# Joined weight half-banks spread over the first routing and the gap ahead of the second layer

## The chip, the cores and the metric

The kernel runs on one NeuronCore of a Trainium2 chip. The metric is the time of one launch in device microseconds; the median of three runs is the time of a kernel. A core has TensorE (PE in the profile), VectorE (DVE), ScalarE (ACT), GpSimd (POOL) and SyncE (SP, here the issuer of most DMAs), which run each its own instruction stream and meet at semaphores.

## The reference

Two layers over 1250 nodes of width 1024, all in float32. Each layer adds to x a graph layer and an attention layer of its normed input, and then a mixture of experts:

```python
edge_index = jnp.stack([src, dst])
xn = _layernorm(x, axis=-1)
x = x + _L0_gnn_ref(xn, edge_index, L0_gnn_W, L0_gnn_b) + _L0_mix_ref(xn[None], ...)[0]
x = x + _L0_ffn_ref(_layernorm(x, axis=-1)[None], L0_ffn_router_gate, ...)[0]
xn = _layernorm(x, axis=-1)
x = x + _L1_gnn_ref(xn, src, dst, ...) + _L1_mix_ref(xn[None], L1_mix_Wq, ..., L1_mix_P)[0]
x = x + _L1_ffn_ref(_layernorm(x, axis=-1)[None], ...)[0]
```

What matters here are two parts. The first expert layer routes: softmax of 8 scores for each token, the best two experts, and in each expert the 391 tokens of largest gate; the kernel must rank the tokens before it can gather any. The attention of the second layer maps queries and keys through a block of 64 features a head before anything else:

```python
q = split_heads(x @ Wq.T + bq)
k = split_heads(x @ Wk.T + bk)
q_prime = _feature_map(q, P)      # relu(q @ P^T) / 8
k_prime = _feature_map(k, P)
```

So Wq and Wk can each be multiplied by P once, ahead of time. These products are the joined weights.

## The kernel before

The work is one long sequence of stages, and the order in each engine's stream is the order in the program text. Matrix products are done as three products of high and low parts (`three`, L515 to L517). Weights come in units of 128 x 2048 (1 MB): SP loads a unit into one of two buffers `WS`, ACT casts the high part into one of two buffers `WH` (`next_unit`, L1494), DVE subtracts to get the low part (L1913), and PE uses the unit. SP's load of a unit waits until the unit two before it has been split.

The joined weights are computed on PE by `joined(n)`, n = 0 to 31 (`JOINED`): block j = n // 2 is one block of 128 rows of Wk (j < 8) or Wq (j >= 8), loaded by SP into `natural(j)`, eight places that the blocks share and that lie in the same memory as the gathered tokens of the experts. A half n is four matmuls against the features `pbd` (L622) into one half of the PSUM tile `PA`. ACT copies each half to `joined_stage(j)`, a ring of `JRING` = 4 places (L1796), SP stores the finished block to the DRAM tensors `pw_d` (`store_joined`, L1196) and then loads the Wq block into the place that is free. Later `linear(pw_d[0])` and `linear(pw_d[1])` load them as weight units.

The first routing, between the graph layer and the experts of layer 0, runs so. DVE computes the gates from the scores (up to L2451) and signals `gates_ready`; PE transposes them (L1041), DVE copies them out (L2458 to L2462); a sum gives the count of each expert. Then for each of 20 groups of tokens PE makes a matrix of all gates (L1056) and DVE compares and counts (L2481 to L2486): the rank loop. From the ranks DVE builds one-hot rows (L2075), PE multiplies them into token numbers (L698), DVE writes `tidx` (L2080), POOL gathers the tokens of expert 0 and, once all joined halves are done, of expert 1 (`gather`, L1423). DVE prepares the gate weights (L2084, L2086) and PE multiplies them (L706). PE then waits for the last copy of a joined half and enters `experts(0)`, which begins with eight register reads and a branch on them, and with the transposes of the gathered tokens (L724).

PE does the joined halves in between: 0 to 5 ahead of the wait for `gates_ready`, 6 to 8 between the transposes, 9 to 21 in the rank loop, 22 to 27 after it, 28 between the two token products, 29 to 31 after them. ACT enters `experts(0)` when all stores have landed.

After the experts PE multiplies the biases by the features (L633, L638), ACT copies them out (L1802, L1804), waits for the last scatter of the experts' results (POOL, L1440) and reads the result back for the second layer; `joined_biases` is the last that the experts' stage leaves on PE before `linear_rows("v1")`.

## Time and profile before

| what | value |
|---|---|
| median of 3 runs | 3187.97 us (3185.45 to 3194.71) |
| the profiled execution | 3187.38 us, of it the span 3185.4 us |
| PE busy | 3002.7 us, 94% of the span |
| DVE, ACT, POOL busy | 62%, 40%, 15% |
| chain that ended last | PE 86%, DVE 7%, issue 2%, DMA 2% |
| granted clock of PE, mean | 0.969 |

The chain is followed back from the last instruction: at each step to what released it. "Issue" is time in which an engine waited for nothing that the profile shows. A busy share is a mean over stages; what a stage is bound by is read in its own window. The routing is short, from about 1024 to 1125 us of the span.

### The profile page before, as it was taken

Reading aid. Unit: us, or ns where it says so; the run is one execution under the profiler, and the core shown is the slowest. Engines: PE = TensorE matmul, PEld = TensorE weight load, DVE = VectorE, ACT = ScalarE, POOL = GpSimd, SP = SyncE. Lnnn points to the kernel's source line nnn. Section 1 sums busy time; section 2 is a strip of 40 time slices with the busy share of each in tenths; the row PEclk is TensorE's granted clock in tenths of the full one; section 3 lists DMA queues with packets and bytes.
Section 4 is the critical chain, followed back from the end, with each engine's and each line's share of the span. In section 5 each row is a group of like instructions: output and inputs, shape, how many; then the busy total and the mean of one; then the engine's idle time right before and its main releaser. Section 6 shows DMA issues by size and latency. Waiting matters only on the chain.

```text
span 3185.4 us, 53094 instructions
## 1 busy us (share of the span) xinstructions
PE 3002.7 (94%) x22248; PEld 2765.1 (87%) x22248; DVE 1983.2 (62%) x3497; ACT 1270.0 (40%) x2176; POOL 462.9 (15%) x328
## 2 busy tenths in 40 slices
PE   8899999999999889999979999999999999979997
PEld 7898898379987778889879999899999999968997
DVE  6986477977876733544456666676355653655665
ACT  3354045444431233433335444544134531424554
POOL 1034443444000111110100000000000000002222
PEclk9999999999999989999989999999999999988999
DMA  7322112123034755755551101363322333248997
GB/s 250 131 59 44 1 16 59 1 51 74 15 86 151 244 142 157 202 154 141 146 148 61 44 27 44 113 153 89 95 78 71 91 90 98 72 137 239 272 281 212
DMA packets 280544, 361.71 MB, mean 114 GB/s; under 512 B 41283, under 2 KB 239465, under 8 KB 278614
## 3 DMA queue, kind: packets, MB, share of 16 engines
q1 hardware_dynamic: 188137, 228.87, 23.6%
q0 software_dynamic: 43312, 77.14, 12.0%
q10 hardware_dynamic: 48829, 51.86, 5.7%
q8 instruction: 203, 3.33, 0.4%
q14 instruction: 63, 0.52, 0.1%
HBM read 273.01 MB, written 84.79 MB: 112 GB/s over the span
## 4 chain that ended last, share of the span: by engine, by line
PE 86%; DVE 7%; issue 2%; DMA 2%; ACT 1%; ACTq 1%; SPq 0%; POOL 0%; DVEq 0%; POOLq 0%
PE PV L515 18%; PE PV L516 18%; PE PV L517 18%; PE PV L685 5%; PE PS L515 3%; PE PS L517 3%; PE PS L516 3%; PE PV L1009 3%; DVE b L2237 2%; PE PA L724 1%; PE PV L915 1%; PE PV L955 1%; PE PA L930 1%; PE PS L930 1%; PE PS L524 1%
## 5 line engine op out<-in xcount | busy, mean ns | idle before, releaser
L515 PE MATMUL PV<-WH,b_split 128*125 128x256 f32 (+2 forms) x4028 | 1174.5, 292 | 41.6 <-DVE b_split L1924 37.1
L516 PE MATMUL PV<-WH,b_split 128*125 128x256 f32 (+2 forms) x4028 | 1159.4, 288 | 2.4 <-issue 2.4
L517 PE MATMUL PV<-WH,b_split 128*125 128x256 f32 (+2 forms) x4028 | 1158.3, 288 | 2.6 <-issue 2.6
L1924 DVE TENSOR_TENSOR b_split<-b,b_split 128x500 fp32r<-128x500 f32 x1008 | 668.7, 677 | 444.5 <-ACT b_split L1504 435.9
L1504 ACT CAST b_split<-b 128x500 fp32r<-128x500 f32 x1008 | 608.4, 613 | 740.9 <-PE PV L517 697.0
L515 PEld LDWEIGHTS PV<-WH,b_split 128*125 128x125 f32 (+2 forms) x4028 | 754.0, 187 | 63.7 <-issue 32.8
L516 PEld LDWEIGHTS PV<-WH,b_split 128*125 128x125 f32 (+2 forms) x4028 | 757.0, 188 | 12.5 <-issue 2.6
L517 PEld LDWEIGHTS PV<-WH,b_split 128*125 128x125 f32 (+2 forms) x4028 | 754.1, 187 | 14.2 <-issue 3.0
L1913 DVE TENSOR_TENSOR WH<-WS,WH 128x1024 fp32r<-128x1024 f32 x292 | 344.4, 1221 | 125.5 <-ACT WH L1494 124.3
L1494 ACT CAST WH<-WS 128x1024 fp32r<-128x1024 f32 x292 | 291.5, 1049 | 182.6 <-PE PV L685 141.1
L1399 POOL DMA_INDIRECT at_d<-ecnt,eidx x168 | 273.9, 1630 | 391.9 <-DMA at_d<-ecnt,eidx 366.7
L1423 POOL DMA_INDIRECT b<-xn_d,tidx x66 | 65.6, 994 | 1611.5 <-issue 1300.1
L515 PE MATMUL PV<-b_split,WH 128*128 128x250 f32 (+3 forms) x816 | 247.5, 303 | 8.2 <-issue 5.9
L516 PE MATMUL PV<-b_split,WH 128*128 128x250 f32 (+3 forms) x816 | 242.5, 297 | 0.0
L517 PE MATMUL PV<-b_split,WH 128*128 128x250 f32 (+3 forms) x816 | 242.0, 297 | 0.0
L685 PE MATMUL PV<-WH,b_split 125*128 125x250 f32 x1600 | 196.4, 286 | 9.6 <-DVE b_split L2040 7.6
L685 PEld LDWEIGHTS PV<-WH,b_split 125*128 125x128 f32 x1600 | 193.5, 194 | 12.5 <-issue 8.0
L515 PE MATMUL PS<-b_split,WH 128*128 128x256 f32 (+2 forms) x496 | 158.6, 320 | 11.2 <-issue 8.4
L515 PEld LDWEIGHTS PV<-b_split,WH 128*128 128x128 f32 x816 | 156.7, 192 | 9.8 <-issue 9.4
L2105 DVE TENSOR_TENSOR b_split<-PA,b_split 128x256 fp32r<-128x256 f32 (+1 forms) x192 | 83.8, 466 | 127.4 <-ACT b_split L1626 127.3
L516 PEld LDWEIGHTS PV<-b_split,WH 128*128 128x128 f32 x816 | 156.9, 192 | 0.2
L517 PEld LDWEIGHTS PV<-b_split,WH 128*128 128x128 f32 x816 | 156.7, 192 | 0.0
(295 smaller groups left out, 3570.3 us busy)
## 6 DMA issues: line engine op xcount, KB each, us to landing
WS<-in_L_ffn_w SPq DMA_DIRECT2D x46, 1024.0 KB, 7.7
WH<-at_d SPq DMA_DIRECT2D x15, 1093.8 KB
WS<-in_L_ffn_gate_w SPq DMA_DIRECT2D x16, 1024.0 KB, 6.6
WS<-in_L_ffn_up_w SPq DMA_DIRECT2D x16, 1024.0 KB, 6.5
WS<-in_L_ffn_down_w SPq DMA_DIRECT2D x16, 1024.0 KB, 5.1
b<-key_d POOLq DMA_DIRECT2D x4, 2560.0 KB, 8.9
WS<-in_L_mix_Wv SPq DMA_DIRECT2D x8, 1024.0 KB, 7.8
WS<-in_L_mix_Wo SPq DMA_DIRECT2D x8, 1024.0 KB, 7.1
```

The lines of the kernel that those rows point to most:

```text
L515: pe.matmul(o, a[0], b[0], start=start, stop=False, **kw)
L516: pe.matmul(o, a[0], b[1], start=False, stop=False, **kw)
L517: return pe.matmul(o, a[1], b[0], start=False, stop=stop, **kw)
L685: mm = pe.matmul(bank[:, 0:AC], part[:, j, f * P:(f + 1) * P].bitcast(dt), at[:, j, :], start=(j + a == 0), stop=(j + a == NT))
L1009: mm = pe.matmul(bank[0:R, :], at[:, j, t * R:(t + 1) * R], part[:, j, half * HALF:(half + 1) * HALF].bitcast(dt), start=(j + a == 0), sto ...
L1399: pool.indirect_dma_start(out=at_d, out_offset=bass.IndirectOffsetOnAxis(ap=eidx[:, g:g + 1], axis=0), in_=ecnt[:, g:g + 1], in_offset=Non ...
L1423: pool.indirect_dma_start(out=ffn_xe(layer, b)[0:r, t, :], out_offset=None, in_=xn_d, in_offset=bass.IndirectOffsetOnAxis(ap=tidx[0:r, c:c ...
L1494: act.copy(WH[:, u.place % 2, a:a + UNIT // 2], WS[:, u.stage % 2, a:a + UNIT // 2])\
L1504: act.copy(hi, src).then_inc(xh_done, 1)
L1913: ve.tensor_tensor(WH[:, u.place % 2, UNIT + a:UNIT + a + UNIT // 2], WS[:, u.stage % 2, a:a + UNIT // 2], WH[:, u.place % 2, a:a + UNIT / ...
L1924: ve.tensor_tensor(lo, src, hi.bitcast(F32), ALU.subtract).then_inc(xl_done, 1)
L2105: ve.tensor_tensor(xeT[:, 1, k, :], bank, xeT[:, 0, k, :].bitcast(F32), ALU.subtract).then_inc(t_free, 1)
```

## The change

The halves are laid out anew. None runs ahead of `gates_ready`; 0 to 2 stand between the transposes, 3 to 16 in the rank loop, 17 to 23 after it, 24 and 25 between the token products. PE then enters the experts after 26 halves (`ROUTED`). The other six, blocks 13 to 15, run after the experts, ahead of the biases. Their Wq blocks, which lay where the tokens of the odd experts are gathered, are loaded by SP after the last transposes of expert 7, and their stores come with the loads of the second layer. The gather for expert 1 waits for 26 halves. The stage ring has three places, so that the late blocks don't touch memory in use. ACT casts the next weight unit ahead of its copies, no longer after six of them, and waits for the late stores ahead of the pieces of the second layer. A block is stored as it lies, 4 KB a partition, and a unit is loaded by two DMAs of one block each, with a semaphore more.

```diff
-JRING = 4
+JRING = 3
 JOINED = 2 * 2 * KD
+ROUTED = 2 * 13
...
-            pe.wait_ge(sm_in, 1)
-            for n in range(6):
-                joined(n)
             pe.wait_ge(gates_ready, 1)
...
-                joined(6 + a)
+                joined(a)
...
-                for m in range(9 + 13 * n // 20, 9 + 13 * (n + 1) // 20):
+                for m in range(3 + 14 * n // 20, 3 + 14 * (n + 1) // 20):
                     joined(m)
             pe.wait_ge(rank_used, rank_ops[2 * NT - 1])
-            for n in range(22, 28):
+            for n in range(17, 24):
                 joined(n)
-            row_tokens(0, lambda: joined(28))
-            for n in range(29, JOINED):
+            row_tokens(0, lambda: [joined(n) for n in range(24, ROUTED)])
+            pe.wait_ge(jw_copied, ROUTED)
+            experts(0)
+            for n in range(ROUTED, JOINED):
                 joined(n)
-            pe.wait_ge(jw_copied, JOINED)
-            experts(0)
             joined_biases()
...
-            def store_joined():
-
-                for j in range(2 * KD):
+            def natural_query(j):
+                sp.dma_start(natural(j), A["L1_mix_Wq"][j * P:(j + 1) * P, :]).then_inc(nat_in[j], 16)
+
+            def store_joined(blocks):
+
+                for j in blocks:
                     sp.wait_ge(jw_copied, 2 * (j + 1))
-                    pr = j % KD
-                    sp.dma_start(pw_d[j // KD][:, pr * P:(pr + 1) * P].rearrange("(k p) c -> p k c", p=P),
-                                 joined_stage(j).rearrange("p (k c) -> p k c", c=P)).then_inc(jw_st[j % JRING], 16)
-                    if j < KD:
-                        sp.dma_start(natural(j), A["L1_mix_Wq"][j * P:(j + 1) * P, :]).then_inc(nat_in[j], 16)
+                    sp.dma_start(pw_d[j // KD][j % KD], joined_stage(j)).then_inc(jw_st[j % JRING], 16)
+                    if j + KD < ROUTED // 2:
+                        natural_query(j)
+
+            def linear_joined(w, vec=None):
+
+                for q in range(NQ):
+                    u = units[n_unit[0]]
+                    n_unit[0] += 1
+                    sp.wait_ge(wl_done, 2 * (u.stage - 1))
+                    for a in range(2):
+                        sp.dma_start(WS[:, u.stage % 2, :].rearrange("p (k n) -> p k n", k=KD)[:, :, a * P:(a + 1) * P],
+                                     w[2 * q + a].rearrange("p (k c) -> p k c", c=P))\
+                          .then_inc(ws_half[u.stage % 2] if a == 0 else ws_full[u.stage % 2], 16)
+                    if vec is not None:
+                        bias(vec, q)
...
-            store_joined()
+            store_joined(range(ROUTED // 2))
...
+            sp.wait_ge(*gather_end[0, E - 1])
+            for j in range(ROUTED // 2 - KD, KD):
+                natural_query(j)
             for q in range(NQ):
                 if q == 2:
+                    store_joined(range(ROUTED // 2, 2 * KD))
                     sp.wait_ge(jw_copied, JOINED + 2)
...
-            linear(pw_d[0], pb_d[0, :])
-            linear(pw_d[1])
+            linear_joined(pw_d[0], pb_d[0, :])
+            linear_joined(pw_d[1])
...
                 if layer == 0:
-                    pool.wait_ge(jw_full, JOINED)
+                    pool.wait_ge(jw_full, ROUTED)
...
-            for slot in range(JRING):
-                act.wait_ge(jw_st[slot], 16 * (2 * KD // JRING))
+            def joined_stored(blocks):
+                for slot in range(JRING):
+                    act.wait_ge(jw_st[slot], 16 * len(range(slot, blocks, JRING)))
+
+            next_unit()
+            for n in range(ROUTED):
+                joined_copied(n)
+            joined_stored(ROUTED // 2)
             experts(0)
+            for n in range(ROUTED, JOINED):
+                joined_copied(n)
...
             next_unit()
+            joined_stored(2 * KD)
             hi_pieces(wide_pieces(B2), lead=lead_x2, order=by_pair)
```

## Rows read from the trace of the kernel before

**Rows 1.** Chain of waits, 1018 to 1150 us: start, duration, what.

```profile
1058.67 1.42 PE PV L1056 x6
...
1097.44 5.84 PE PA L622 x48
1103.29 1.79 PE PV L698 x20
...
1107.13 4.97 PE PV L706 x40
1112.10 4.69 PE PA L622 x24
...
1117.41 7.37 issue
```

**Rows 2.** Timeline of PE: start, duration, instruction, in brackets the idle before.

```profile
1042.01 8.37 PE L622 MATMUL PA<-b 128*128 128x128 f32 x48 [3.65 <-DMA b<-in_L_mix_Wk]
...
1055.85 1.23 PE L1041 MATMUL PV<-ident,RB 125*8 125x125 f32 x10
```

**Rows 3.** Timeline of DVE: start, duration, instruction, in brackets the idle before.

```profile
1044.60 0.24 DVE L2451 TENSOR_TENSOR RB<-RB 125x80 f32<-125x80 f32 x1
1051.27 0.67 DVE L2460 CAST b_split<-PV 8x500 fp32r<-8x500 f32 x1 [6.42 <-PE PV L1041]
...
1102.00 2.41 DVE L2075 TENSOR_TENSOR b_split<-RB,rowno 125x490 fp32r<-125x490 f32 x4
1105.11 0.19 DVE L2080 TENSOR_SCALAR tidx<-PV 98x32 int32<-98x32 f32 x1 [0.70 <-PE PV L698]
```

**Rows 4.** Timeline of POOL: the memset and the last gather of expert 0.

```profile
1038.43 4.26 POOL L1405 MEMSET b_split<- 128x5000 f32 x1 [227.60 <-PE PA L552]
...
1109.86 0.95 POOL L1423 DMA_INDIRECT b<-xn_d,tidx  x1 [0.30 <-issue]
```

**Rows 5.** Windows: busy of PE, PEld, DVE, ACT, POOL, then clock, DMA share, GB/s.

```profile
1040.50:1041.00 0.50, 0.00 (x0) 0.00 (x0) 0.50 (x9) 0.00 (x0) 0.50 (x1) 0.90 1.01 393
1047.50:1048.00 0.50, 0.50 (x5) 0.50 (x5) 0.00 (x0) 0.49 (x1) 0.00 (x0) 0.78 1.08 442
1119.00:1119.50 0.50, 0.00 (x0) 0.00 (x0) 0.00 (x0) 0.00 (x0) 0.27 (x1) 0.90 0.98 261
1133.00:1133.50 0.50, 0.50 (x5) 0.50 (x4) 0.32 (x1) 0.15 (x1) 0.00 (x0) 0.94 0.00 0
```

**Rows 6.** DMA: landings of gathers at 1109.86 and 1120.83; listing 1020 to 1130 us.

```profile
DMA to landing us min/median/max: 5.9/5.9/5.9
DMA to landing us min/median/max: 12.4/12.4/12.4
...
pw_d<-b SPq DMA_DIRECT2D x16, 512.0 KB, 3.4
b<-in_L_mix_Wq SPq DMA_DIRECT2D x8, 512.0 KB, 7.0
WS<-in_L_ffn_up_w SPq DMA_DIRECT2D x1, 1024.0 KB, 15.1
```

**Rows 7.** SP, ACT, chain and one window between the experts and the second layer.

```profile
1553.28 7.23 SPq L1178 DMA_DIRECT2D WS<-in_L_ffn_down_w  x2
...
1589.40 0.17 ACT L1804 COPY bcol<-PA 128x8 f32<-128x8 f32 x1 [1.30 <-PE PA L638]
...
1588.92 8.16 DMA x_d<-b,sidx
...
1588.00:1590.00 2.00, 1.36 (x13) 1.28 (x12) 0.00 (x0) 0.27 (x2) 1.70 (x2) 1.00 0.99 172
```

**Rows 8.** Second layer: a load of joined weights, its cast, landings of such loads.

```profile
1712.81 0.43 SPq L1178 DMA_DIRECT2D WS<-pw_d  x1
...
1744.94 1.99 ACT L1494 CAST WH<-WS 128x1024 fp32r<-128x1024 f32 x2
...
DMA to landing us min/median/max: 4.8/5.7/7.7
```

13 lines of the change are left out of this document (8 added, 5 removed).

## Prediction

> **What bounds the kernel now.** I read the page first: TensorE (PE) is busy 94% of the span and holds 86% of the chain of waits, so time is won only where that chain leaves the long runs of matmuls. Then I read the chain of waits from 1018 to 1150 us, the first routing, where all 32 half-banks of joined weights (L622, one `joined(n)` each) are computed. PE's own timeline [rows 2] shows six of them at 1042.01 for 8.37 us, after 3.65 us of waiting for the Wk blocks. The chain [rows 1] holds six more at 1097.44 for 5.84 us (0.97 each); three at 1112.10 for 4.69 us. Then the timelines of DVE and POOL in the same stretch [rows 3, 4], to see who waits behind PE; the granted clock in half-microsecond windows [rows 5]; the DMA listing and the landings [rows 6]; the chain, ACT and the DMA between the experts and the second layer, where six halves go [rows 7]; and the loads of the joined weights in the second layer [rows 8].
>
> **The profiled execution.** It took 3187.38 us for a span of 3185.4; the median of three runs is 3187.97. I work in differences against the profiled one and take them off the median.
>
> **Front of the routing.** DVE finishes the gates at 1044.60 + 0.24 = 1044.84 and then idles 6.42 us until 1051.27 [rows 3], because PE stands in the six halves until 1042.01 + 8.37 = 1050.38 [rows 2] before it transposes the gates. The change takes these six out. The other input of that step, POOL's memset, ends at 1038.43 + 4.26 = 1042.69 [rows 4], so the gates are last: PE can start at 1044.84 in place of 1050.38, 5.5 us earlier. All the halves that stay between the gates and the first rank matmul (three) are the same number as before.
>
> Against it stands the clock. It fell to half during the 3.65 us in which PE waited for Wk and came back at about 1047.7, after PE had been kept full by the six halves [rows 5]. Now PE idles some 6.5 us and meets the transposes at half clock, 1.2 GHz in place of 2.4. From 1050.38 to 1058.67 [rows 1] PE has some 6.5 us of work at full clock (30 transposes, of which ten take 1.23 us [rows 2], and three halves of 0.97); the rest of the 8.3 us is DVE's. If the clock returns about 5 us after the start, the PE work is some 2.5 us behind, of which DVE's share hides about 1: a cost of 1.5. If it returns within 3 us the cost is under 1; if only at the rank matmuls, 2 x 6.5 - 8.3 = 4.7, or a little more. I take 1.5: PE is kept nearly as full as it was by the six halves, if with smaller matmuls. Front: 5.5 - 1.5 = 4.0, between 0.5 and 5.
>
> The Trainium skill ("TensorE: Matmul & The Clock Gate", section "HAM oscillation — how this bites in real kernels") says that gaps in PE's work return it to half rate and that each burst after one begins cold. The trace agrees: the pauses of 3.65 and 7.37 us both ended at half clock [rows 5].
>
> **Rank loop.** From 1058.67 to 1097.44 DVE is busy without a break worth naming; PE does 14 halves beside it in place of 13. Where three steps in a row now carry one, PE's step is about as long as DVE's (38.8/20 = 1.94): cost 0.3, bounds 0 and 0.9 (a whole half).
>
> **Between ranks and tokens.** Seven halves in place of six: 7 x 0.97 = 6.8 us. The first token matmul follows the halves at once, at 1103.29 [rows 1], when DVE's last one-hot is still being written (1102.00 + 2.41 = 1104.41 [rows 3]); the 20 matmuls of 1.79 us end at 1105.08 and tidx is written at 1105.11. In the new order the halves end so late that nothing of this hides: cost 1.0, bounds 0 and 1.0.
>
> **Tail.** Under DVE's weights (1105.11 to 1107) two halves run in place of one. They take 1.9 us and DVE 2.0: nothing, or 0.9 if the cover is gone. After the weight matmuls (L706, 4.97) the three halves and the last copy, 1112.10 to 1117.41, fall away: 5.3. The 7.37 us "issue" behind them stays whole. In the code it is eight register reads and a branch, all behind the wait for the copies, and the first gather had landed by then: 1109.86 + 5.9 = 1115.8 [rows 4, 6]. What is late next is this gather: with tidx 2.7 earlier its last tile lands near 1113, PE wants it at 1116.8.
>
> **Ring of three and SP.** ACT now waits for the store three blocks back. A block takes 1.9 us of halves, so three take 5.8, and a store lands in 3.4 [rows 6]: covered; without cover each block would cost the difference, up to 1.5. ACT's weight cast goes ahead of its copies (2 us, in PE's pause). SP leaves the stores for the expert weights 5 us earlier or more.
>
> First routing: 4.0 - 0.3 - 1.0 + 5.3 = 8.0 us.
>
> **The six moved halves.** PE ends the experts near 1585.6, ACT its bias copies at 1589.40 + 0.17 = 1589.57 [rows 7]. With six halves of about 0.95 between them ACT ends near 1595.1. ACT's next step waits for the last scatter, 1588.92 + 8.16 = 1597.08 [rows 7]: covered by 2 us. If the halves ran at half clock this cover is gone and 3 us would come on top. Blocks 5 to 7 of Wq are read again by SP after its last expert weights, issued by 1553.28 + 7.23 = 1560.5; such a block takes 7.0 us to land [rows 6], PE wants them at 1585.6: covered by 18 us. The Wv loads queued behind them on SP wait for a buffer anyway.
>
> What is not free is the stores of blocks 13 to 15: SP issues them at about 1588, 1590 and 1592, 1.5 MB through the engines that the scatter fills to 0.99 at 172 GB/s [rows 7]. The nearest rows: the last tile of the gather that ran beside the 1 MB up_w load landed in 12.4 us, that of the one before it in 5.9, and up_w took 15.1 [rows 6]. So sharing can cost up to 6.5; down to 0 if the scatter has only latency to wait for. I take 3: only part of the stores lies ahead of the scatter's last packets. The chain runs through this landing, so it counts in full.
>
> The Trainium skill ("DMA: Bandwidth & Descriptors", section "Queues, rings and completion order") has each DMA engine take turns between its queues packet by packet. By it the scatter gives up half of the engines as long as stores are queued; a rule without it would let the scatter, issued earlier, go first and the cost be near 0.
>
> **Blocks of 4 KB a partition.** Stores get longer pieces; loads of the joined weights become two DMAs with 512 B pieces on chip. A load is issued at 1712.81, lands in 7.7 at most and is cast at 1744.94 [rows 8]: even at twice the time it is 16 us early. Nothing; the same for ACT's new waits ahead of the second layer, since the stores land before the scatter's successor loads do.
>
> **Sum.** 8.0 - 3.0 = 5.0 us: 3182.4 for the profiled execution, 3183.0 for the median.
>
> **Rivals.**
> 1. The scatter is not held. For: its landings may be latency. Against: up_w and the gather both grew. Gain 8.0: 3180.0.
> 2. The clock stays low through the front. For: a longer pause, and the half-clock spell from 1119 to 1133 outlasted the first 8 us of work [rows 5]. Against: at 1047.7 it returned after 5.7 us. Front 0.5 in place of 4.0: gain 1.5, 3186.5.
> 3. The gather becomes the late one: gather(1) now follows at once, no longer held by the last half, beside the stores. With 12.4 in place of 5.9 its predecessor's last tile lands at 1107.2 + 12.4 = 1119.6, 2.8 after PE wants it: gain 2.2, 3185.8. Against: it lies ahead of gather(1) in its queue.
> 4. Slower: the stores hold the scatter by their whole size. 1.57 MB at the 172 GB/s of that stretch are 9.1 us; 8.0 - 9.1 = 1.1 lost, 3189.1. It decides from 8.0 us of delay on. Against: these bytes need no read of the target, and the nearest row shows 6.5.
>
> **Chances.** Forecast 0.50, rivals 0.20, 0.12, 0.10 and 0.08. The clock at either routing end may add or take 2.5 us (the half-clock spell at the start of the experts can fall otherwise). With it the ends are a gain of 11.5 (rival 1 with a good clock) and a loss of 2: 3176.5 to 3190. A change of 0.3% is 9.6 us, about what a measurement tells from none. Faster by more: half of rival 1, a tenth of the forecast and a little of the rest, 0.17; slower by more: part of rival 4, 0.05; within: 0.78.
>
> **What would show it.** Right: the gate transposes begin within 0.5 us of gates_ready; DVE's 6.4 us gap is gone; the first expert transpose (L724) comes 7 to 9 us earlier; the last scatter before the second layer lands in 10 to 13 us, not 8.2. Wrong: a gap of DVE in the rank loop, PE released into the experts by a gather, ACT's bias copies after the scatter, or any wait of ACT for a joined load. The prediction fails most easily at the scatter and at the clock.

## The result and the profile after

The changed kernel takes 3169.2 us (median of 8 runs, 3165.7 to 3171.2) against 3186.2 us (median of 8, 3180.1 to 3194.7): a ratio of 0.9943, interval 0.9931 to 0.9954. It is 17 us faster where 5 were forecast, and 7 us under the low end of the range. Its profiled execution took 3169.48 us, of it the span 3167.7, against 3187.38 and 3185.4 before.

The difference of the two spans, 17.7 us, stage by stage (each border is the start of the named instruction of PE in either trace):

| stage | before | after | difference | forecast |
|---|---|---|---|---|
| start to the last scores | 1038.1 | 1035.9 | -2.2 | 0 |
| last scores to first gate transpose | 12.1 | 6.8 | -5.3 | -5.5 |
| to the first rank matmul | 8.5 | 9.0 | +0.5 | +1.5 |
| to the first token product (L698, now L701) | 44.3 | 45.4 | +1.1 | +1.3 |
| to the first expert transpose (L724, now L727) | 21.8 | 15.0 | -6.8 | -5.3 |
| experts, to the end of PE's expert matmuls | 460.8 | 448.8 | **-12.0** | **0** |
| to the key products of the second layer | 186.9 | 191.6 | +4.7 | +3 |
| to the end | 1412.9 | 1415.2 | +2.3 | 0 |

The first and the last row are no work of the change. Over the profiles of all kernels below whose code is the same up to there, the last scores began between 1035.3 and 1042.0 us; and the last row came to 1410.7 us in a second profile of the changed kernel and to 1411.9 in one of the kernel before. So single rows of this table are good to a microsecond or two where they are short, and to a few where they are long. The routing and the stage behind the experts came out near the forecast. Most of what the forecast lacked is one line, the experts, none of whose instructions the change touches.

The chain of waits of the changed kernel, answering [rows 1] (start, duration, what):

```profile
1090.61 6.74 PE PA L625 x56
1097.34 1.68 PE PV L701 x20
...
1103.79 8.20 DMA b<-xn_d,tidx
```

The halves behind the rank loop are seven, 6.74 us. The three halves and the 7.37 us of "issue" that ended the routing are gone from the chain; it ends with the landing of a gather. PE's timeline says the same, and answers [rows 2] (in brackets the idle time before, and its releaser):

```profile
1042.69 2.25 PE L1041 MATMUL PV<-ident,RB 125*8 125x125 f32 x10 [6.53 <-DVE RB L2479]
...
1101.07 3.62 PE L709 MATMUL PV<-RB,b_split 125*98 125x32 f32 x40 [0.18 <-DVE RB L2114]
1112.13 1.54 PE L727 MATMUL PA<-ident,b 98*128 98x98 f32 x8 [7.44 <-DMA b<-xn_d,tidx]
```

DVE's timeline, answering [rows 3]: the gates are ready at 1042.63, the gap behind them is 1.51 us where it was 6.42, and `tidx` waits 1.47 us for the token product, where it waited 0.70:

```profile
1042.39 0.24 DVE L2479 TENSOR_TENSOR RB<-RB 125x80 f32<-125x80 f32 x1
1044.14 0.67 DVE L2488 CAST b_split<-PV 8x500 fp32r<-8x500 f32 x1 [1.51 <-PE PV L1041]
...
1099.05 0.19 DVE L2108 TENSOR_SCALAR tidx<-PV 98x32 int32<-98x32 f32 x1 [1.47 <-PE PV L701]
```

Windows of the changed kernel (length, busy of PE, PEld, DVE, ACT, POOL, granted clock, DMA share, GB/s), answering [rows 5]:

```profile
1047.00:1047.50 0.50, 0.50 (x5) 0.29 (x3) 0.47 (x2) 0.28 (x1) 0.00 (x0) 0.56 1.06 410
1047.50:1048.00 0.50, 0.50 (x6) 0.42 (x5) 0.50 (x2) 0.00 (x0) 0.00 (x0) 1.00 0.99 350
...
1118.00:1119.00 1.00, 1.00 (x5) 1.00 (x4) 0.44 (x1) 0.00 (x0) 0.00 (x0) 0.50 1.04 246
1119.00:1120.00 1.00, 1.00 (x8) 0.90 (x8) 0.00 (x0) 0.34 (x1) 0.00 (x0) 0.94 0.62 140
```

PE began the gate transposes at 1042.69 at half clock (1.2 GHz) and had the full one (2.4 GHz) from 1047.5, 4.8 us later; it began the experts at 1112.13 at half clock and had the full one 6.9 us later.

Between the experts and the second layer, answering [rows 7]: chain of waits, then ACT's timeline (its last line stands in the chain as well), then SP's.

```profile
1564.30 12.20 DMA x_d<-b,sidx
```

```profile
1570.36 0.17 ACT L1831 COPY bcol<-PA 128x8 f32<-128x8 f32 x1 [1.30 <-PE PA L641]
...
1587.60 1.28 ACT L1543 ACT_TABLE_LOAD   x1 [4.51 <-DVE b L2007]
```

```profile
1563.46 5.34 SPq L1199 DMA_DIRECT2D pw_d<-b  x3
```

ACT's bias copies end 9.7 us behind PE's experts (9.5 forecast) and are covered by the scatter. The scatter, with three stores of joined blocks issued from 0.8 us ahead of it on, lands in 12.20 us where it landed in 8.16. And a step stands in the chain that was not in it before: ACT's table load for the square root. The loads of the joined weights, answering [rows 8], now of half the size, land in 6.1 us at the median, where those of 1 MB took 5.7, and nothing waits for them:

```profile
WS<-pw_d SPq DMA_DIRECT2D x10, 512.0 KB, 6.1
```

**Where the 12 us of the experts went.** One window over the stage, of the kernel before and of the changed one:

```profile
1124.80:1585.60 460.80, 444.31 (x2495) 391.94 (x2496) 202.18 (x254) 169.47 (x254) 70.81 (x54) 0.98 0.57 155
```

```profile
1112.10:1560.87 448.77, 441.16 (x2495) 389.83 (x2496) 201.94 (x253) 169.44 (x254) 70.63 (x54) 0.99 0.60 164
```

The same 2495 matmuls. PE's idle time falls from 460.80 - 444.31 = 16.5 to 7.6 us, that is by 8.9, and its busy time by 3.1, at a mean clock of 0.99 in place of 0.98. What PE waited for in this stage, before and after (us in total, times, longest):

```profile
PE PV L515 <- issue: 5.9, 3, 5.3
PE PS L515 <- issue: 5.5, 2, 3.0
PE PV L517 <- issue: 2.6, 1, 2.6
```

```profile
PE PS L518 <- issue: 2.6, 1, 2.6
PE PS L520 <- issue: 1.3, 1, 1.3
PE PV L520 <- issue: 0.5, 1, 0.5
PE PV L518 <- issue: 0.5, 1, 0.5
```

PE stands still with nothing to wait for, 14.0 us before and 4.9 after. The largest stops of the kernel before, in PE's timeline and in the chain:

```profile
1149.47 0.67 PE L515 MATMUL PV<-b_split,WH 128*128 128x392 f32 x1 [5.30 <-issue]
```

```profile
1248.42 2.56 issue
...
1292.87 2.43 issue
...
1341.47 3.04 issue
```

They fall between matmuls whose data were there. For the longest that needs a second look, since DVE splits a weight unit until 1148.03, shortly before PE goes on at 1149.47, and in one of the kernels below (a_pad24) the profile names this split as the releaser of the same stop. But in the changed kernel PE begins the same matmul at 1130.88, and DVE begins that split only at 1132.42: it is of a later unit. What moves at that moment is the instruction queue. It shows 39 transfers in the stage, and each of the four stops has one. In the three shorter stops it starts within 0.3 us of the stop, takes about 1 us, and PE goes on 1.5 to 2.1 us after its end; in the longest it starts at 1146.6, 2.4 us into the stop.
```profile
q8 instruction: 1, 0.02, 11.8%
```

The longest stop also costs clock. Windows of the kernel before, columns as above:

```profile
1146.00:1148.00 2.00, 0.00 (x0) 0.00 (x0) 2.00 (x2) 0.59 (x1) 0.00 (x0) 0.68 0.79 213
...
1150.00:1152.00 2.00, 2.00 (x8) 2.00 (x7) 0.00 (x0) 0.00 (x0) 0.00 (x0) 0.50 1.08 378
...
1154.00:1156.00 2.00, 2.00 (x16) 1.96 (x14) 0.12 (x1) 0.00 (x0) 0.00 (x0) 1.00 0.00 0
```

At half clock PE did 8 matmuls in two microseconds, at the full one 16. The DMA engines were busy in most of these stops, but not in all: in the one from 1248.4 to 1251.0 their share is 0.23 in this trace.

The Trainium skill ("Runtime: NRT & Kernel Launch", section "Instruction fetch mechanics") says that each engine's instructions are fetched in blocks of 16 KiB, 256 instructions, while it executes the current ones, that the cost of crossing into a new block is mostly hidden, and that a taken branch breaks the fetching ahead. The size agrees with the 16.4 KB of a transfer here. "Mostly hidden" doesn't hold for this stage as a whole, with 13.3 us in four stops. What branches have to do with it is the last experiment's question.

So the theory behind the experiments: **the change moved 24 matmuls (six halves of four) from ahead of the experts to behind them, and thereby the place of every instruction of the experts within its block. Where the block's borders fall decides how long PE waits for the next block.** The rival: the moved work itself, or the times of the gathers, makes the experts faster.

### The profile page after: what moved, and what is told of

It is laid out like the page before. It is cut to its first block, busy times and chain, and to the rows that moved or that the text cites. A ratio compares the mean times of both kernels' runs of the same rounds, so it can differ in the third digit from the quotient of the medians.

```text
span 3167.7 us, 53105 instructions
## 1 busy us (share of the span) xinstructions
PE 2990.9 (94%) x22248; PEld 2754.0 (87%) x22248; DVE 1982.6 (63%) x3497; ACT 1270.0 (40%) x2176; POOL 468.0 (15%) x328
## 3 DMA queue, kind: packets, MB, share of 16 engines
q0 software_dynamic: 43312, 77.14, 12.1%
## 4 chain that ended last, share of the span: by engine, by line
PE 88%; DVE 6%; issue 2%; ACT 1%; DMA 1%; ACTq 1%; SPq 0%; POOL 0%; DVEq 0%; POOLq 0%
PE PV L518 18%; PE PV L520 18%; PE PV L519 18%; PE PV L688 6%; PE PS L518 4%; PE PS L520 3%; PE PS L519 3%; PE PV L1012 3%; PE PA L727 2%; DVE b L2265 2%; PE PV L918 1%; PE PV L958 1%; PE PA L933 1%; PE PS L933 1%; PE PS L527 1%
```

## The experiments

**Repeats** (b_again, a_again). Both kernels again, for what is chance.

> The kernel before, unchanged, profiled once more. Between the first expert transpose and the biases PE stood idle four times for 5.3, 2.6, 2.4 and 3.0 us with nothing to wait for, each with an instruction transfer in flight. If the stops belong to where the instructions lie, they come back at the same instructions and with about the same size; if they are chance, they come elsewhere or are smaller.

> The changed kernel, unchanged, once more: 3169 us, ratio 0.994. In its first trace only two such stops stood in the experts, 1.3 and 2.6 us. By the layout theory the same two return; by chance the sum could be anything up to the 13 us of before.

The kernel before took 3187.6 us, its stage of experts 463.2. The changed kernel took 3166.4 us, ratio 0.9937 (0.9913 to 0.9962), its stage 449.9. Large stops of similar size stood at the same places of either stage (5.5, 3.0, 2.6 and 2.1 us; 1.2 and 2.4). They belong to the program and not to the run.

**The place alone, in both directions.** Matmuls of two columns, of whose result nothing is used. In f32 each is four instructions of PE, as those of a joined half are. First at the start of PE's stream: 24 in the changed kernel (a_pad24), which puts the experts where those of the kernel before lie, and 40 in the kernel before (b_pad40), 24 + 40 = 64 matmuls or 256 instructions from the changed kernel.

```diff
             pe.wait_ge(consts, 8)
+            for _ in range(24):
+                pe.matmul(PA[0:P, 0, 0:2], ident[:, :], ones[:, 0:2], start=True, stop=True)
```

> The changed kernel with 24 small matmuls at the very start of PE, where PE is idle for the first 30 us. They cost nothing there, but put the expert instructions back to the place that they had before the change (the six moved halves are 24 matmuls). Layout theory: the stops of before return (5.3 us at the first hidden columns, 13 us in all in place of 4) and the time is 3178 us. Rival (the stop of 5.3 us came from the transfers beside it, or from chance): no change, 3169 us.

> The kernel before with 40 such matmuls at the start: the expert instructions lie as in the changed kernel, if what counts is their place within blocks of 16 KB. Layout theory: 9 us less, 3177 us. Rival: as before, 3186 us.

The changed kernel with 24: 3182.8 us, ratio 0.9989 (0.9978 to 1.0000), experts 463.1. The kernel before with 40: 3178.8 us, 0.9976 (0.9964 to 0.9987), experts 447.7. The expectation that these matmuls are free was wrong. The 24 took 10.4 us, so that PE's first transposes began at 14.5 us in place of 12.4, and the 40 took 17.2 us and put them off from 12.0 to 21.4. The last scores came 3.6 and 8.2 us later; the first of these lies within what they move by themselves (1035.3 to 1042.0), the second doesn't. But the stage of experts changed sides in both kernels.

Then the same in the routing, 40 ahead of the first joined half of the kernel before (b_gap40) or 24 ahead of the wait for the gates in the changed kernel with its table load mended (t_gap24; the mending is a_table's, below):

```diff
+            pe.wait_ge(sm_in, 1)
+            for _ in range(24):
+                pe.matmul(PA[0:P, 0, 0:2], ident[:, :], ones[:, 0:2], start=True, stop=True)
             pe.wait_ge(gates_ready, 1)
```

> The kernel before with forty matmuls of two columns (their result is used by nobody) behind PE's wait for sm_in, ahead of the first joined half, where PE waits 3.6 us for the weights of Wk in the kernel before. They shift the place of every later instruction of PE as forty such matmuls at the start of PE did (which shortened the experts from 461 to 448 us but cost 10 us at the start), and do nothing else to the routing. Theory (the place of PE's instructions sets 13 of the 17 us): the stage from the first expert transpose to the end of PE's expert matmuls is 448 us instead of 461 to 463, the routing is 0 to 3 us longer by the forty matmuls, and the whole is 3186.5 - 13.5 + 1.5 = 3174.5 us, 3172.5 to 3176.5. Rival (the forty at the start did it by something else than their place, such as by when x0's loads or the scores ran): experts 461 to 463 us, whole 3186 to 3190 us.

> The changed kernel with the table load mended as in the run on that, and twenty-four matmuls of two columns ahead of PE's wait for the gates, where PE stands idle. Their number is that of the matmuls of the six halves that the change moved behind the experts, so the experts' instructions of PE lie where those of the kernel before lie. Theory of the place: the experts' stage is 463 us instead of 449, the front is no longer than in the changed kernel (at most 1 us either way, for the clock falls later), and the whole is 3168 + 13.5 = 3181.5 us, 3179.5 to 3183.5: the gain of the moved work alone, about 5 us of 3186.5, which is what was forecast for it. Rival (the moved halves themselves make the experts faster): experts 449 us and 3168 us.

The kernel before with 40: 3184.8 us, 0.9996 (0.9984 to 1.0009), experts 446.3. The total is 10 us above the expected one, since the 40 cost 11.7 us here and not 1.5. Each took 0.39 us, nearly all at half clock. The changed kernel with 24: 3187.6 us, 1.0002 (0.9990 to 1.0015), experts 462.5. That is 6 us above the expectation; 3.2 of it is the cost of the 24 ahead of the gates, and the rest is open: the profiled execution, from which the stages are read, took 3177.6 us, 10 less than the median. The window over its experts and three of the stops in its chain (the longest, 5.3 us, is back as well, at the same matmul as in the kernel before):

```profile
1115.20:1577.74 462.54, 445.74 (x2495) 393.26 (x2495) 202.09 (x253) 169.34 (x254) 70.58 (x54) 0.97 0.60 160
```

```profile
1237.63 2.50 issue
...
1283.35 2.75 issue
...
1333.57 2.60 issue
```

They stand 122.4, 168.2 and 218.4 us behind the first expert transpose (1115.2). In the kernel before it is 123.6, 168.1 and 216.7 (from 1124.8).

**Is it the place within a block?** In the same place a whole block, 64 matmuls, and two other values, each profiled once.

 Theory of the block: every later instruction lies at the same place within its block as in the changed kernel, and the experts' stage (first expert transpose to the end of PE's expert matmuls, 448.8 us in the changed kernel, 462.5 with twenty-four) is 448 to 452 us, with the stops for issue at the instructions of the changed kernel (the largest near 204 us into the stage). Rival (any matmuls ahead of the experts lengthen the stage, or more of them more so): 462 us or above. The sixty-four cost some 22 to 25 us ahead of the gates (0.39 us each, as forty took 15.8 us in b_gap40), so that the whole is 3190 us by the theory and 3204 by the rival; the stage alone is what tells.

> As t_gap24 with twelve matmuls of two columns: 48 instructions, half of the way from the places of the changed kernel to those of the kernel before. Theory of the block, in which each block's end meets another matmul and other transfers of the weights: the stage is anything between 448 and 463 us, and its stops stand at other matmuls than in either kernel. Rival (a switch between two states by some threshold): 448 or 463 us to within 2 us, with the stops of one of the two kernels. The whole is 3168 us plus what the stage has above 449 (the twelve lie in PE's idle time).

> As t_gap24 with forty-four matmuls of two columns: 176 instructions, between the places of the kernel before (24) and the whole block (64). Theory of the block: the stage is between 446 and 465 us, with stops at other matmuls. Rival (more matmuls ahead, longer stage): above 463 us. The forty-four cost some 11 us ahead of the gates.

With 64, window and stops:

```profile
1133.60:1579.95 446.35, 439.55 (x2494) 388.23 (x2495) 201.90 (x253) 169.58 (x254) 71.35 (x55) 0.99 0.62 166
```

```profile
1292.06 1.26 issue
...
1337.93 1.31 issue
```

The short stage is back, with stops 158.5 and 204.3 us behind the first transpose (1133.6). The changed kernel has them at 158.6 and 204.5 (from 1112.1):

```profile
1270.67 1.34 issue
...
1316.62 2.63 issue
```

So what counts is neither that matmuls are added nor how many, and the remainder in blocks of 256 instructions fits. Half, a quarter or an eighth of a block as the period doesn't: 12 and 44, which lie half a block apart, differ by 10.7 us in the table. By the matmuls that stand ahead of the experts beyond those of the changed kernel:

| matmuls more | kernel | stage of experts | of it PE idle | PE busy |
|---|---|---|---|---|
| 0 | changed | 448.8 | 7.6 | 441.2 |
| 0 | a_table | 451.7 | 9.8 | 441.9 |
| 8 | a_28 | 458.7 | 13.2 | 445.5 |
| 12 | t_gap12 | 462.2 | 16.9 | 445.3 |
| 24 | before | 460.8 | 16.5 | 444.3 |
| 24 | a_pad24 | 463.1 | 17.9 | 445.2 |
| 24 | t_gap24 | 462.5 | 16.8 | 445.7 |
| 44 | t_gap44 | 451.5 | 8.5 | 442.9 |
| 64 | b_pad40 | 447.7 | 7.1 | 440.6 |
| 64 | b_gap40 | 446.3 | 6.1 | 440.2 |
| 64 | t_gap64 | 446.4 | 6.8 | 439.6 |

The kernels that are not in the table keep to their side: 462 to 463 us in b_again, b_front and b_4k (24 more), 448 to 450 in a_again, a_held, a_hoist and a_late (none more). The expectation for twelve was half wrong: three of its four large stops do not stand at other matmuls. They stand at 18.9, 163.5 and 213.9 us into the stage, where the kernel before has three of its own. The fourth, 3.05 us at 440.6, has no counterpart there. With 8 the stage lies between the two values; with 44 it is that of a_table, with one large stop (3.8 us) in place of a_table's two of 1.3 and 2.9. The whole times of the three single runs (3185.8, 3180.4 and 3177.1 us) carry the added matmuls too and say less.

**The front alone** (b_front). The kernel before with the halves of the routing spread as in the change, but the last six left behind the weight products, ahead of the experts. The places of the experts' instructions stay.

```diff
-            pe.wait_ge(sm_in, 1)
-            for n in range(6):
-                joined(n)
...
-                joined(6 + a)
+                joined(a)
...
-                for m in range(9 + 13 * n // 20, 9 + 13 * (n + 1) // 20):
+                for m in range(3 + 14 * n // 20, 3 + 14 * (n + 1) // 20):
...
-            row_tokens(0, lambda: joined(28))
-            for n in range(29, JOINED):
+            row_tokens(0, lambda: [joined(n) for n in range(24, 26)])
+            for n in range(26, JOINED):
```

> The kernel before with one part of the change alone: no half-bank ahead of the gates, 3, 14, 7 and 2 at the later places as in the change, and the last six still ahead of the experts, after the weight matmuls. The expert instructions lie as before, so the layout theory gives the stops of before and an experts stage of 461 to 463 us, not 448. The front gains 5, six halves after the weight matmuls cost 6 in place of three for 5: in all 3 to 4 us gained, 3183. If instead the front itself brought the missing gain, 3175 or less.

ACT casts the next weight unit ahead of its copies here, too. 3185.9 us, 1.0001 (0.9987 to 1.0015), where 3183 were expected: no gain is seen, though the interval leaves room for one of 4 us. Between the scores and the gate transposes it wins 5.3 us, as the changed kernel does, but six halves now stand between the weight products and the experts where there were three, and the first expert transpose comes only 0.6 us earlier against the scores. Experts 463.0. By this trace the front is worth something only with the six halves taken away.

**What releases the experts.** First the second gather held back until the experts have begun (a_held), then also PE's eight register reads moved into the rank loop (a_hoist).

```diff
                 if layer == 0:
                     pool.wait_ge(jw_full, ROUTED)
+                    pool.wait_ge(t_full, 1)
                 gather(1)
```

```diff
+                if n in (3, 5, 7, 9, 11, 13, 15, 17):
+                    pe.wait_ge(nsel_ready, 1)
+                    e = len(chosen)
+                    chosen.append(pe.value_load(nsel[0:1, e:e + 1], min_val=0, max_val=T))
                 if n >= 2:
                     pe.wait_ge(rank_used, rank_ops[n - 2])
```

> The changed kernel, but the gather for expert 1 waits until PE has turned the first bank of expert 0, so that it no longer runs beside the gather of expert 0. In the changed kernel the last tile of that gather landed in 8.2 us (5.9 before) and the first expert transpose came 7.4 us after the weight matmuls, at the very moment of landing. If the gather sets the start (rival 3 of the prediction), the transpose comes 2 us earlier and the kernel gains 2 us. If the eight register reads and the branch set it (7.4 us before as after), nothing moves: 3167 us.

> As a_held, and the eight register reads are made one by one between the steps of the rank loop. If the 7.4 us are these reads, the first transpose now waits for the gather alone, some 5 us after the weight matmuls: 2 us gained, less what the reads delay the rank loop (0 to 5 us, if each takes 0.6 us of PE). If they are the branch, nothing is gained.

3166.4 us, 0.9939 (0.9923 to 0.9956), and 3169.4 us, 0.9951 (0.9934 to 0.9967): neither differs from the changed kernel. PE's timeline of the first and of the second:

```profile
1116.72 1.54 PE L727 MATMUL PA<-ident,b 98*128 98x98 f32 x8 [5.74 <-DMA b<-xn_d,tidx]
```

```profile
1111.82 1.54 PE L727 MATMUL PA<-ident,b 98*128 98x98 f32 x8 [5.49 <-DMA b<-xn_d,tidx]
```

With the reads out of the way PE still waits 5.5 us, for the gather's landing; with them in their place it waited 5.7 us in a_held and 7.4 in the changed kernel. So what comes last there is the gather, and taking the reads away alone is worth nothing. How far behind the gather the reads would hold PE is not measured. The gather's landing moved between 4.9 and 8.2 us, also with the second gather held: that gather is not what it waits for.

**The scatter.** In a_late the three late stores are put behind the read-back of x2, so that the scatter runs without them, and ACT waits for them behind the first pair of the second layer.

```diff
                 if q == 2:
-                    store_joined(range(ROUTED // 2, 2 * KD))
...
                     sp.dma_start(gate_sb[:, :, :], A["L1_ffn_gate_w"].rearrange("(k p) e -> p k e", p=P))\
                       .then_inc(rg1_in, 16)
+                    store_joined(range(ROUTED // 2, 2 * KD))
```

> The changed kernel, but the stores of blocks 13 to 15 wait until the first rows of the result are back, and ACT waits for them after the first pair of the second layer in place of ahead of it. Theory: the last scatter lands in 8.2 us again in place of 12.2 (4 us), and ACT's table load falls back into its pause (1.3 us): 5 us less than the changed kernel, 3163. Rival: the landing of the scatter grew for another reason, and the stores now delay the rows that come back: no gain or a loss.

3177.3 us, 0.9972 (0.9959 to 0.9985): 8 us worse than the changed kernel. The scatter in the chain, and the stores in the DMA listing (the last number there is the median from issue to landing):

```profile
1565.05 8.03 DMA x_d<-b,sidx
```

```profile
pw_d<-b SPq DMA_DIRECT2D x3, 512.0 KB, 20.1
```

The scatter is back at 8.0 us: its 4 us are the stores' doing. But beside the read-back and a load of Wv the stores themselves take 20 us and become the late thing: the chain waits 19.5 us for them. The other way to less of it, a_28, is two late stores in place of three, with the two halves more behind the weight products, under the gather (the table load is mended, as in a_table below):

```diff
-ROUTED = 2 * 13
+ROUTED = 2 * 14
...
-            row_tokens(0, lambda: [joined(n) for n in range(24, ROUTED)])
+            row_tokens(0, lambda: [joined(n) for n in range(24, 26)])
+            for n in range(26, ROUTED):
+                joined(n)
```

> The changed kernel with the table load mended and four of the 32 halves instead of six behind the experts: the two others stand behind the matmuls of the combine weights, where PE waits 5 to 7 us for the gather; two joined blocks instead of three are stored beside the last scatter. Theory: the scatter lands in some 11 us instead of 11.2 to 12.2 (8.2 without late stores, plus two thirds of 4), the two halves (1.8 us) lie in the wait for the gather, so that the first expert transpose is no later than with six; 0 to 2 us of gain with the experts at the same length. But the eight matmuls move the experts' instructions by 32 places, so that their stage may be anything between 447 and 463 us: whole 3167 to 3182 us. The stage tells which. Rival: the gather waits for the two halves (pool waits for all the halves ahead of the second gather) and the first expert transpose comes 2 us later: nothing gained.

3179.5 us, 0.9971 (0.9957 to 0.9984), 10 us worse, 7 to 10 of them in the experts, which take 458.7 us by the place of their instructions. PE also stood 3.1 us for issue behind the gather's landing, ahead of the first transpose, so that this came 2 us later than without the two halves. The scatter landed in 11.18 us, no sooner than in other runs with three late stores (10.7 to 12.2). Two stores hold it as well as three, or this difference is too small to see.

**The table load** (a_table). ACT's waits for the last stores one line higher:

```diff
-            next_unit()
-            joined_stored(2 * KD)
+            joined_stored(2 * KD)
+            next_unit()
```

> The changed kernel with one wait moved: ACT's waits for the three last stores of joined weights (joined_stored(2 * KD)) stand ahead of next_unit() instead of behind it. In the changed kernel ACT's table load of 1.28 us (L1543) starts at 1587.60, when DVE's L2007 is done, because these waits and the one for the variance stand ahead of it. Theory: with the waits ahead of the weight casts the table load lies in ACT's idle time ahead of the variance again, as before the change, and the stage from the end of the experts to the key products is 1.3 us shorter than the 191.8 us of the changed kernel; 3167.9 us. The stores land before the scatter does, so that moving their wait forward holds nothing. Rival: the waits now hold the weight casts (L1515, 1.05 us, that follow the scatter), and nothing is won: 3169.2 us. No instruction of PE moves, so the experts stay at 448 to 450 us by either.

ACT's line for the square root in this kernel (durations least, median, most in ns; first and last start):

```profile
L1543 ACT ACT_TABLE_LOAD  x1: 1283/1283/1283, 1585.1 to 1585.1; - x1
```

The load now starts 4.4 us ahead of the square root that needs it (1589.5) and is gone from the chain. The stage from the end of PE's expert matmuls to the key products is 190.5 us (191.6), as expected. The time is 3168.9 us, 0.9944 (0.9924 to 0.9964): one microsecond doesn't show in medians that differ by 3.

**The 4 KB layout alone** (b_4k), with the store into whole tiles and the waits for both halves of a load.

```diff
-        pw_d = [dram("pw_d0", [D, D]), dram("pw_d1", [D, D])]
+        pw_d = [dram("pw_d0", [KD, P, D]), dram("pw_d1", [KD, P, D])]
...
-            linear(pw_d[0], pb_d[0, :])
-            linear(pw_d[1])
+            linear_joined(pw_d[0], pb_d[0, :])
+            linear_joined(pw_d[1])
```

> The kernel before with the third part of the change alone: the joined weights are stored as whole tiles of 4 KB a partition and loaded back in two halves of 512 B pieces a square with a wait for each. PE's instructions are the same ones at the same places. Theory (forecast: nothing): stores and loads lie under other work, and the time is that of the kernel before, 3186.5 us, 3184.5 to 3188. Rival: the loads of joined weights in the second layer (sixteen of 512 KB where eight of 1 MB were) land sooner or later than those before, and as the weight casts wait for them, the time from the end of the experts to the key products moves by 1 to 3 us: 3183.5 or 3189.5 us.

3188.3 us, 1.0001 (0.9989 to 1.0012). From the end of the experts to the key products it takes 186.1 us, as before (186.9). This part does nothing.

**Which blocks are late?** The stops keep to few places. The windows from the first transpose to a stop count PE's matmuls up to it, first in the kernel before (two of four), then in the changed one:

```profile
1124.70:1144.10 19.40, 16.75 (x92) 15.50 (x92) 5.58 (x10) 6.84 (x13) 3.73 (x4) 0.78 0.45 113
...
1124.70:1248.30 123.60, 115.46 (x644) 106.06 (x644) 50.01 (x68) 44.38 (x72) 17.61 (x16) 0.94 0.54 149
```

```profile
1112.10:1270.70 158.60, 155.97 (x907) 141.07 (x908) 71.08 (x94) 60.85 (x96) 27.35 (x24) 0.98 0.61 163
1112.10:1316.70 204.60, 200.57 (x1194) 180.43 (x1194) 95.65 (x125) 81.20 (x126) 37.24 (x31) 0.98 0.64 171
```

The other two of the kernel before stand at 896 and 1194. In the code each step of an expert is written out twice, for three and for four tiles of tokens, and PE jumps over one of the two by a branch (`sized`, L840 to L857 in the changed kernel). The first gate has 92 matmuls and transposes, a hidden step 164, the gate of the next expert 60, a down product 96 or, with three tiles, 74. With the sizes of this input (the third and fourth expert have three) the steps begin at 0, 92, 256, 316, 412, 576, 636, 732, 896, 956, 1030, 1194. So 92, 896 and 1194 are the first matmuls behind a jump, and 644 and 907 stand 8 and 11 behind one. The first of these stops also shows the border of a block moving. Windows from the first transpose into the stop, with 12 and 8 matmuls more, then of b_pad40, which is a whole block from none:

```profile
1116.90:1135.90 19.00, 16.31 (x93) 14.92 (x94) 5.57 (x10) 7.32 (x15) 4.01 (x5) 0.83 0.66 160
```

```profile
1115.50:1136.00 20.50, 17.88 (x101) 16.15 (x101) 7.01 (x12) 9.18 (x16) 3.78 (x4) 0.83 0.60 147
```

```profile
1133.00:1157.00 24.00, 21.38 (x117) 19.86 (x117) 8.51 (x14) 9.22 (x16) 3.79 (x4) 0.83 0.52 133
```

The stop stands behind 93, 101 and 117 matmuls. Each of these is two instructions of PE (its weight load and itself), each added one four. So 4 matmuls less ahead, 16 instructions, put the stop 8 matmuls later, and 8 less, 32 instructions, 16 later: just what a border at a fixed number of instructions does. With 24 it would stand behind 69, ahead of the jump at 92, and there PE stops at the jump itself. The stop is the shorter the farther the border lies behind the jump: 5.3 us at 92 and at 93, 3.0 at 101, 1.2 at 117. In these four (before, t_gap12, a_28, b_pad40) PE goes on at nearly the same time, 5.9, 6.3, 5.9 and 6.3 us behind the start of the last four transposes ahead of the jump (4.6 to 6.5 over all kernels with this stop). So at this jump the next block seems to come at a time of its own, and PE stands still for what is left of it.

Then the jumps were taken out, in the changed kernel with its table load mended:

```diff
                 def sized(b, step):
-                    if layer == 1:
-                        step(tiles)
-                        return
+                    step(tiles)
+                    return
```

> The changed kernel with the table load mended, in which PE always runs the version of four tiles of each step of the first experts and no longer chooses between three and four by a branch. The other engines run four tiles anyhow, so nothing else changes. Cost: three experts of eight run three tiles today; in the kernel before the hidden stage of one of them takes 21.2 us where one of four tiles takes 27.6, its gate 7.5 for 9.3, its down product 17.3 for 22.7, so the stage grows by 3 x 13.6 = 41 us, and the whole is some 3205 to 3212 us. Theory (PE stops where it jumps over a version and the block of the target, or the one behind it, is not there yet): no stop of over 0.5 us for issue between the first expert transpose and the end of the experts; PE idle in the stage at most 4 us where it is 9.8. Rival (each crossing into a new block can be late, branch or not): stops of 1 to 3 us remain, in all 4 us or more.

> As t_flat, with twenty-four matmuls of two columns ahead of the wait for the gates, which with the branches lengthened the stage of experts from 449 to 462 us. Theory: without the branches the place doesn't count, the stage is that of t_flat within 2 us and has no stop of over 0.5 us. Rival: it is 5 us or more longer than in t_flat, with stops of 2 to 3 us. The whole is that of t_flat and 3 us.

The windows over the experts of t_flat and of t_flat24:

```profile
1112.80:1595.43 482.63, 480.06 (x2560) 424.56 (x2561) 203.56 (x254) 169.53 (x254) 71.17 (x56) 0.99 0.57 154
```

```profile
1113.10:1594.83 481.73, 479.16 (x2561) 423.72 (x2562) 203.58 (x254) 169.54 (x254) 70.22 (x55) 0.99 0.57 154
```

PE is idle for 2.6 us in either, no stop for issue is left, and the stage is 482.6 and 481.7 us: without jumps the two places make no difference. The instruction queue over the stage of the kernel before and of t_flat (transfers, MB, share):

```profile
q8 instruction: 39, 0.64, 0.6%
```

```profile
q8 instruction: 21, 0.34, 0.3%
```

The code that is written twice and jumped over brings 18 transfers more. PE's busy time grew by 38.2 us (41 expected) and its idle time fell by 7.2, which the expected 41 did not take off. The whole times, of one run each, were 3192.3 and 3195.4 us, where 3205 to 3212 were expected. Blocks that are reached straight on are there in time, here at all the borders of a stage of 2560 matmuls. So the stops need both: a jump, and a place of its target that makes PE enter a block too soon behind it. t_flat takes out the jumps and the second version of the code together, so that the two are not told apart by it. The section of the Trainium skill named above says that a taken branch whose target isn't held stalls PE until its block is fetched, and the stops at the jumps bear that out.

## Why the prediction was wrong

**The step that failed** is one that the sum doesn't have: it ends at the first expert transpose and begins again behind the experts, and takes the 461 us between as unchanged. They fell by 12.0 us in the profiled pair, and moved by 11 to 15 in the kernels with added matmuls. The stops were in the trace of before, four of them, 13.3 us, at matmuls that waited for no data; the prediction read the experts only at their ends. It also weighed the clock there, 2.5 us for the half-clock spell at the start, and not the second spell of some 7 us behind the stop at 1144 us. Whether the stops would grow or shrink could not have been read from that trace, but that the change moves 96 instructions and so changes them could. The right form would have been a term with a low end of about -14, all stops gone, and a high end above nothing, and a range that wide; over all kernels with jumps the stage then took 446.3 to 463.2 us, 14.5 less to 2.4 more than the 460.8 of before.

**The change's own work came out as forecast.** Scores to first expert transpose: 86.7 us before, 76.2 after, a gain of 10.5 for 8.0 forecast. By step:
- Gate transposes 5.3 us earlier for 5.5; the clock took 0.5 back, not 1.5. It returned 4.8 us after PE's start (forecast "about 5"), but the three halves and DVE's share hid more of it.
- Rank loop and ranks to tokens: +1.1 for +1.3. `tidx` waits for the halves as the forecast said.
- Tail: -6.8 for -5.3. The step "7.37 us of issue stays whole" was right in size (7.44) and wrong in cause: it now ends with the gather, which by a_hoist takes 5.5 us even where the register reads are out of the way. The rest is the weight products, 3.62 us for 4.97. They ran wholly at full clock here, while it had fallen to 0.58 by 1109 to 1110 us in the kernel before. They took 4.46 and 4.18 in a_held and a_hoist, so part of it is chance.
- Rival 3 (the gather is late), also one of the prediction's own signs of being wrong, is what is seen, but without its price: the gather lands near 1112.0, and a_hoist found nothing to gain in having PE ready sooner.

**The scatter**: +4.0 us (12.20 for 8.16; 10.7 to 12.2 over the kernels with late stores) for +3, within 0 to 6.5. a_late shows that the stores cause it. Rival 1 (not held) and rival 4 (held by 9.1) fall.

**Missed on the way**: ACT's table load. The waits for the stores were costed at nothing because the stores land early. That was right for the wait. But in ACT's stream the table load stands behind whatever waits are written between it and the instruction before, and the new waits and the one for DVE's variance went ahead of it. So 1.28 us came into the chain, as a_table shows.

**Covered steps** that held: the six halves' copies (9.7 us for 9.5), Wq's three late blocks, the ring of three, the 4 KB layout.

Together: routing 10.5 - behind the experts 4.7 = 5.8 us for 5.0 forecast, and 12.0 from the experts. The two kernels that take the experts' part away don't contradict this, but they are too coarse to confirm it. With 24 at the start the gain is 3.5 us (0 to 7), and the added matmuls put off PE's start by 2.2 us: some 6 together, if that carries through to the end. With 24 ahead of the gates it is -0.6 (-4.8 to +3.2) and they cost 3.2: 2.6 together, of which about 1 belongs to the mended table load.

**What stays open**: why the large stops nearly all lie in the first 220 us of the stage, though the jumps go on to its end (t_gap12 has one of 3.05 us at 440.6 us, a_again one of 1.6 at 433), what the first 2.4 us of the longest stop are, and how many blocks PE holds, which would say in advance which jump is late. A kernel with fewer jumps (one for each expert in place of three or four) was not tried; it may keep the three-tile version and lose most of the stops.

## What to carry to other kernels

Where an engine's long program has branches, every edit ahead of them moves their targets and can change the time of a stage that it doesn't touch; compare such stages first, and repeat the kernel with as many idle instructions as the edit took out before the difference is put down to the edit. Such instructions cost time themselves, so read the stage and not the whole. A stop that the profile calls "issue" near a branch belongs in the forecast as a term with bounds on both sides. A wait that is satisfied early can still cost, by what is ordered behind it.

## What the runs showed of the hardware

- PE was idle 16 to 18 us in a stage of 461 to 463 at one place of the code and 6 to 10 us at another, for the same matmuls, and 2.6 us at both without jumps. The short stage and its stops came back after 256 instructions, and with 16 and 32 instructions less ahead the first stop moved by just as many.
- At one jump PE went on 4.6 to 6.5 us after the start of the last four transposes ahead of it, whatever it still had to do before the block's border: the stop was 5.3 us right behind the jump and 1.2 us 25 matmuls behind it.
- A matmul of two columns in f32 is two passes. In b_gap40 eleven passes fell into the microsecond from 1043 us at full clock (granted clock 1.00), and 25 into the five from 1050 at half clock (0.50), 0.4 us a matmul. PE was busy with them without a pause from 1042.8 us, and yet the clock fell to half at about 1044.4 and stayed there until about 1061.4, 3 us into the joined halves. Such padding isn't free.
- A scatter that lands in 7.8 to 8.2 us without late stores lands in 10.7 to 12.2 beside two or three of 512 KB, and these take 20 us beside a read-back and a weight load.
- Single runs of the kernel before on one chip lay between 3179.8 and 3198.0 us (25 runs), those of the changed kernel between 3165.7 and 3171.2 (8 runs).
